# The last subtraction in rounding the gate weights: from GpSimd to VectorE

## Reference

```python
def _mx_dequant(t):
    rows, feat = t.shape
    blocks = t.reshape(rows, feat // _BLOCK, _BLOCK)          # _BLOCK = 32
    max_abs = jnp.max(jnp.abs(blocks), axis=-1)
    scales = jnp.maximum(max_abs / _FP8_MAX, _EPS)
    q = (blocks / scales[..., None]).astype(jnp.float8_e4m3fn).astype(jnp.float32)
    return (q * scales[..., None]).reshape(rows, feat)
gate = _mx_dequant(x2d) @ _mx_dequant(gate_w).T
up = _mx_dequant(x2d) @ _mx_dequant(up_w).T
out = _mx_dequant(silu(gate) * up) @ _mx_dequant(down_w).T
```

## Time and profile before

| | us |
| --- | --- |
| runs of the kernel before | 564.76, 558.96, 564.05 |
| their median | 564.05 |
| the profiled execution | 558.41 |
| its span (first to last instruction) | 556.6 |
| mean granted TensorE clock in it | 0.972 of full speed |

### The profile page before, as it was taken

The page is one execution under the profiler, slowest core; times in us unless marked ns, Lnnn a source line. Parts: engine busy times, 40 slices in busy tenths (PEclk is TensorE's granted clock), DMA queues, the critical chain, the costliest instruction groups (busy, mean ns, idle before and its releaser), DMA issues.

```text
span 556.6 us, 9598 instructions
## 1 busy us (share of the span) xinstructions
PE 482.3 (87%) x3265; PEld 317.1 (57%) x3265; DVE 363.7 (65%) x785; ACT 232.0 (42%) x627; POOL 230.9 (41%) x244
## 2 busy tenths in 40 slices
PE   2775188778999999999999999999989899969896
PEld 1654143546755667666557576665667666646542
DVE  3798978668977848787694678858833562321435
ACT  1463042224552352466535325653442255533452
POOL 1243253387664484332123642311354331216285
PEclk9997599999999999999999899999999999988999
DMA  7970040044312122022221000232111035321001
GB/s 285 330 307 0 4 146 0 5 140 151 113 53 96 48 86 58 0 60 57 69 90 39 21 1 8 61 95 60 48 38 39 1 94 149 96 78 42 1 1 38
DMA packets 38255, 41.82 MB, mean 75 GB/s; under 512 B 7168, under 2 KB 33408, under 8 KB 37312
## 3 DMA queue, kind: packets, MB, share of 16 engines
q1 hardware_dynamic: 33840, 36.50, 20.7%
q10 hardware_dynamic: 4080, 3.93, 2.0%
q0 software_dynamic: 288, 0.79, 0.5%
HBM read 34.13 MB, written 7.08 MB: 74 GB/s over the span
## 4 chain that ended last, share of the span: by engine, by line
PE 65%; DVE 18%; SPq 5%; ACT 5%; issue 3%; POOL 2%; DMA 1%; ACTq 0%; DVEq 0%; POOLq 0%
PE qc L748 16%; PE s L748 11%; PE ga L748 10%; PE qb L748 10%; PE ua L748 6%; PE tp L751 5%; PE tp L748 3%; DVE reg L1439 3%; DVE amax L1288 2%; DVE simwk L1386 1%; SPq L671 1%; ACT reg L1191 1%; SPq L716 1%; SPq L666 1%; PE ga L751 1%
## 5 line engine op out<-in xcount | busy, mean ns | idle before, releaser
L1687 POOL TENSOR_TENSOR reg<-reg,rsum 128x512 f32<-128x512 f32 x64 | 66.1, 1048 | 145.7 <-DVE rsum L1452 145.6
L1101 ACT COPY reg<-tp 128x512 f32<-128x512 f32 (+1 forms) x100 | 51.1, 511 | 75.3 <-PE tp L751 58.4
L1191 ACT ACTIVATE reg<-s,nmax 128x256 f32<-128x256 f32 x128 | 59.4, 475 | 43.9 <-DVE nmax L1445 43.9
L748 PE MATMUL qb<-reg,wA_hi 128*128 128x256 f16 x384 | 69.0, 275 | 3.6 <-DVE reg L1439 1.9
L748 PE MATMUL qc<-reg,wM 128*64 128x256 f32 (+1 forms) x384 | 66.5, 391 | 4.5 <-DVE reg L1439 3.9
L1445 DVE TENSOR_REDUCE nmax<-s 128x2 f32<-128x512 f32 x64 | 42.1, 681 | 42.3 <-PE s L748 42.3
L751 PE MATMUL tp<-idn,reg 128*128 128x128 f32 x296 | 49.4, 287 | 7.5 <-ACT reg L1101 5.9
L748 PEld LDWEIGHTS qc<-reg,wM 128*64 128x64 f32 (+1 forms) x384 | 37.3, 154 | 25.2 <-issue 13.6
L751 PEld LDWEIGHTS tp<-idn,reg 128*128 128x128 f32 x296 | 34.0, 144 | 26.0 <-issue 17.5
L748 PEld LDWEIGHTS qb<-reg,wA_hi 128*128 128x128 f16 x384 | 35.0, 99 | 20.3 <-issue 7.3
L1439 DVE TENSOR_TENSOR reg<-qb,cosq 128x768 f32<-128x768 f32 x32 | 30.5, 955 | 19.7 <-PE qb L748 14.7
(11 more groups left out here) (224 smaller groups left out, 901.9 us busy)
## 6 DMA issues: line engine op xcount, KB each, us to landing
masks<-in_moe_masks SPq DMA_DIRECT2D x16, 512.0 KB, 3.9
wtile<-wE_d SPq DMA_DIRECT2D x120, 64.0 KB, 1.8
y_d<-masks ACTq DMA_DIRECT2D x15, 256.0 KB, 2.2
wM<-in_att_wq SPq DMA_DIRECT2D x1, 2048.0 KB, 8.2
wtile<-in_wo_t SPq DMA_DIRECT2D x1, 2048.0 KB, 17.9
wE_d<-moe SPq DMA_DIRECT2D x16, 128.0 KB, 2.5
reg<-in_kc_q SPq DMA_DIRECT2D x1, 1536.0 KB, 11.2
reg<-in_qr_t SPq DMA_DIRECT2D x1, 1536.0 KB, 13.5
```

Source lines behind the costliest of these rows:

```text
L748: return nc.tensor.matmul(dst, lhsT, rhs, start=start, stop=stop, skip_group_check=not check)
L1101: nc.scalar.copy(dst, src).then_inc(bank.drained, 1)
L1191: nc.scalar.activation(attn[p % 2][:, (2 * hh + t) * S:(2 * hh + t + 1) * S], s.tensor[:, t * S:(t + 1) * S], ACT.Exp, bias=nmax[:, o:o + ...
L1687: nc.gpsimd.tensor_tensor(a, a, rsum[:, o:o + 2].unsqueeze(2).to_broadcast([P, 2, S]), ALU.mult).then_inc(attn_ready.sem, 1)
```

## The change

For the gate matrix (m = 0), VectorE makes the subtraction that ends the rounding, straight behind the addition in `quant_w(0, 2)`, as it did for m = 1 only. `dequant_w(0)` on GpSimd no longer subtracts: it waits for one step of VectorE more and scales. For m = 2 GpSimd still does both. The semaphore values follow.

```diff
-        w0 = [0, 7, 15, 22]
+        w0 = [0, 8, 16, 23]
         w_step = count("w_step", 0, w0[-1])
-        w_rounded = count("w_rounded", 0, 2)
+        w_rounded = count("w_rounded", 0, 1)
@@ quant_w, VectorE
-                if m == 1 and part == 2:
+                if m < 2 and part == 2:
                     dve.wait_ge(w_step.sem, w0[m] + 7)
                     nc.vector.tensor_tensor(nat[m], nat[m], wmag[m], ALU.subtract).then_inc(w_step.sem, 1)
@@ dequant_w, GpSimd
                 pool.wait_ge(w_step.sem, w0[m + 1])
-                if m != 1:
+                if m == 2:
                     nc.gpsimd.tensor_tensor(nat[m], nat[m], wmag[m], ALU.subtract).then_inc(w_rounded.sem, 1)
-                    pool.wait_ge(w_rounded.sem, 1 + m // 2)
+                    pool.wait_ge(w_rounded.sem, 1)
                 dequant(w_ready, nat[m], nat[m], wscale[m % 2], 64)
```

## The result

| | us |
| --- | --- |
| kernel before, median of 22 runs (557.98 to 566.69) | 561.21 |
| changed kernel, median of 22 runs (553.50 to 563.42) | 559.01 |
| ratio of the changed kernel to the one before | 0.9935, 95% interval 0.9910 to 0.9961 |
| profiled execution of the changed kernel, and its span | 556.96, 555.2 |

The change makes the kernel 0.65% faster, 3.6 us of 561.2 us, with an interval of 2.2 to 5.1 us. The ratio leaves disturbed, slow runs out; over all runs the medians differ by 2.2 us and the means by 3.3 us. With 22 runs instead of three, the times of the kernel before are spread over 558 to 567 us, with none between 561.6 and 563.4 us; the runs of the later series fill that gap too, so the three that were shown before lay in two places by chance.

A forecast was written before the change was run, and what follows sets the result against it. The prediction took VectorE's setup chain, held by GpSimd at two maskings, as the bound. Its terms, -4.26 us and -0.43 us, taken as 4.7 us off 564.05 us, gave 559.35 us, range 553.0 to 562.5 us.

The forecast's parts named there:

- What bounds the stretch, and that GpSimd holds the maskings: Setup, 31.9 to 64.6 us: VectorE's chain bounds; GpSimd's subtraction and scaling stretch two L1386 maskings to 8.2 us.
- VectorE's added 2.33 us: Behind the gate weights' addition ending at 34.18 us: the new subtraction puts 2.33 us into VectorE's chain.
- GpSimd's scaling ends the stall, first masking 0.28 us and second 0.69 us behind it: Batch 0 maskings: GpSimd's scaling ends at 40.90 us, the maskings at 41.18 and 41.59 us.
- Memsets not held: GpSimd's two memsets at 35.22 us lose nothing beside VectorE's new subtraction; rival that they are held: 3.4 us off, chance 0.09.
- Clock term, 0.43 us: TensorE's adjacency turn: shorter idle time keeps the clock full, four blocks take 0.65 instead of 1.08 us, 0.43 us off.
- After it, everything moves by the same distance: Behind the adjacency turn to the end: all work starts 4.7 us earlier; rival that loops absorb this: 564.05 us, chance 0.11.
- such a shrinking as a sign of being wrong: Between 65 us and the end: the prediction is wrong if the distance of 4.7 us shrinks there.
- The size, 4.7 us: Whole kernel: 4.26 us from VectorE's chain and 0.43 us from TensorE's clock, taken as 4.7 us off, chance 0.75.
- Before, the pair ended at 45.85 us: Batch 0 maskings in the kernel before: end at 45.85 us, against 41.59 us with the change, a gain of 4.26 us.
- The runs' level: Three runs of the kernel before read as two levels, 558.96 us and 564.05 and 564.76 us, with the same gain at both.
- the predicted 559.35 us: Whole kernel: the median of three runs, 564.05 us, less 4.7 us, which is -0.83%.

The follow-up runs named there:

- the half-scaled kernel: Changed kernel with GpSimd scaling only the first 1024 of the gate weights' 2048 columns; ratio to the kernel before 0.9932.
- the second execution of the changed kernel: Changed kernel, unaltered, timed and profiled once more beside the kernel before; ratio 0.9915, span of its profile 552.8 us.
- the kernel with the pass kept: Changed kernel with GpSimd again making a subtraction, into a scratch tile, ahead of its gate scaling; ratio to the kernel before 1.0042, repeated 1.0043.
- the matmuls: Changed kernel with 48 idle matmuls on TensorE ahead of turn_w(1, 0); ratio to the kernel before 0.9909, repeated 0.9902.
- all subtractions on VectorE: Changed kernel with the down weights' subtraction (m = 2) moved to VectorE too; ratio to the kernel before 0.9940, with 48 idle matmuls 0.9921.

## Why the prediction was right, and where a term was off

The mechanism was right; the size of one term is doubtful, and that the predicted time lies so close to the measured one is partly luck.

- *What bounds the stretch, and that GpSimd holds the maskings:* right. Both ends follow GpSimd when its work is lengthened, shortened or halved.
- *VectorE's added 2.33 us:* right to 0.01 us (32.29, 34.62 and, for the maximum behind it, 36.83 us), and it costs nothing while the stall is there.
- *GpSimd's scaling ends the stall, first masking 0.28 us and second 0.69 us behind it:* 41.76 us and 42.43 us, right (0.67 us).
- *Memsets not held:* right, in the half-scaled kernel with an overlap of 1.6 us. The Trainium skill, page "SBUF — State Buffer", section "Who interferes with whom", has the rule that a VectorE instruction with two inputs in SBUF doesn't contend with a GpSimd instruction that only writes it. The 1.95 us of the memsets and the 2.29 us of the subtraction agree with this rule, and not with the plain reading of the same section that whoever holds the shared ports blocks the other.
- *Clock term, 0.43 us:* right. The turn took 0.63 us (in the first profile at a clock of 1.00), and L1394 followed 0.74 us after its start instead of 1.19 us.
- *After it, everything moves by the same distance:* right as far as 250 us, for the work behind the clock's return. The turns of the adjacency on TensorE in the next batches start at 148.95, 249.52 and 356.12 us in the kernel before, at 144.25, 244.82 and 349.80 us in the second execution of the changed kernel: 4.70, 4.70 and 6.3 us earlier. In the first execution it is 2.4, 2.4 and 4.0 us, because of its 3.85 us the clock's late return took 1.45 us (11.08 against 9.63 us). At the end 3.8 and 1.4 us are left. The prediction named such a shrinking as a sign of being wrong; but the distance first grows and then shrinks, in stretches where the mean granted clock is below 1.00 in one kernel and not in the other (0.97 in the kernel before from 310 to 360 us; 0.97 in both of the changed kernel from 410 to 460 us, and 0.96 and 0.95 from 510 to 552 us). So it goes with the clock; that it is only the clock isn't shown.
- *The size, 4.7 us:* by the profiles this term was mis-sized. The step that failed is "Before, the pair ended at 45.85 us", taken as what the kernel before always does. It is its long course only, decided by 0.38 us between two starts that I had in my rows (37.26 and 37.64 us) and didn't question. Up weights in the long course: 49.79 us (49.83 and 50.15 us in the kernel with the pass kept, which was in it both times); in the short one: 47.83 us. The changed kernel and its kin with the matmuls or all subtractions on VectorE reach them at 45.93, 44.99, 45.37, 46.30, 45.75 and 44.99 us, 45.6 us on average. With nine parts long and five parts short the kernel before would be at 49.2 us on average, and the gain 3.6 us: an estimate from these profiles. The time doesn't decide it. The first series gives 3.6 us, the second 4.8 us, and the predicted 0.83% lies within the intervals of both.
- *The runs' level:* I read two levels out of three runs; 22 runs show a spread. That the predicted 559.35 us lies 0.3 us from the measured median is luck: the reference median sank by 2.8 us, from 564.05 to 561.21 us, and the medians differ by 2.2 us instead of 4.7 us, and the two nearly cancel.
- *Open:* the kernel with the pass kept is 0.42% above the kernel before in two series, 2.4 us. If it always goes the long way, that explains 49.92 - 49.2 = 0.7 us of it (49.92 us is the mean of the three long ones above). The rest, at the edge of the intervals, isn't explained; its first 50 us hold no further loss.

## What to carry to other kernels

Where GpSimd works in SBUF for several us, look at which VectorE instructions with two SBUF operands stand beside it, and compare the duration of each with the same instruction elsewhere. Here the stretched ones were held, and they ended 0.3 us (128x256) or 0.55 us (128x512) behind a GpSimd instruction; where that is so, moving work onto VectorE can be free or better. Before you subtract such a stall, look at how far apart the two instructions start; if it is less than their starts scatter, the stall is there only in a part of the executions, and only that part can be won. The sum then needs several profiles of the kernel before, one isn't enough.

## What wasn't expected of the hardware

- A held VectorE instruction can get in between two GpSimd instructions that follow one another at 0.07 us: the first masking did, at 41.78 us, and GpSimd's next took 3.70 us instead of 3.64 us. L1398, issued 0.28 us after the second of a pair had started, was held for all of it (3.90 us).
- A small lead decides much: with GpSimd 0.38 us ahead both maskings were stretched, to 4.42 and 3.85 us; with VectorE 0.03 us ahead only the second was, to 4.75 us.
- TensorE's granted clock can also be low right after short idle times and while it is busy: in the first execution with the 48 matmuls it was 1.00 up to 44 us and stood at 0.53 from 44 to 46 us, with TensorE busy for all of the 2.00 us, after idle times of 1.3 and 0.9 us at 41 to 44 us. In the first profile of the changed kernel, after the same idle times, it was 1.00 from 44 to 45 us.

```profile
44.00:46.00 2.00, 2.00 (x18) 1.57 (x16) 1.93 (x8) 0.00 (x0) 0.46 (x1) 0.53 0.00 0
```
